# Causal attention with two layer norms: column maxima and sums on VectorE, a third score bank

## The reference, cut to what matters

```python
cq = rms_norm(x @ w_qa.T, q_ln)                       # 2048 x 384
q = (cq @ w_qb.T)                                     # 16 heads x (128 + 64)
ckv = x @ w_kva.T                                     # 128 compressed + 64 rotary
scores = einsum(q_full, k_full) * 192 ** -0.5         # per head 2048 x 2048, causal
attn = softmax(where(causal, -inf, scores))
x = layernorm(x + (attn @ v).reshape(s, H * 128) @ w_o.T)
x = layernorm(x + x @ (weight * scale_weight[:, None]).T + bias)
```

## Time and profile before

| | |
|---|---|
| median of 3 runs | 1709.2 us (1709.2 to 1710.53) |
| profiled execution, its own time | 1709.03 us |
| span of its trace | 1707.2 us |
| TensorE busy | 1648.9 us (97%) |
| VectorE busy | 1399.1 us (82%) |
| ScalarE busy | 1102.1 us (65%) |
| GpSimd busy | 983.7 us (58%) |
| granted TensorE clock | 0.998 |

### The profile page before, as it was taken

The page is one execution under the profiler, slowest core; times in us unless marked ns, Lnnn a source line. Parts: engine busy times, 40 slices in busy tenths (PEclk is TensorE's granted clock), DMA queues, the critical chain, the costliest instruction groups (busy, mean ns, idle before and its releaser), DMA issues. The chain is left out here.

```text
span 1707.2 us, 27648 instructions
## 1 busy us (share of the span) xinstructions
PE 1648.9 (97%) x8405; PEld 1355.0 (79%) x8405; DVE 1399.1 (82%) x2499; ACT 1102.1 (65%) x2064; POOL 983.7 (58%) x937
## 2 busy tenths in 40 slices
PE   7999999999999999999999999999999999999887
PEld 5667788888888888888887878888888788888665
DVE  3565798888888888888888888888888988888895
ACT  4554576666666666766666666766666767666664
POOL 4333465565655556656566555655655665565795
PEclk9999999999999999999999999999999999999999
DMA  7984322212321412223211312123113121111322
GB/s 218 367 319 145 97 68 63 87 58 87 112 79 38 143 37 81 69 80 124 81 56 59 127 58 92 50 81 118 62 63 113 43 70 49 50 44 56 118 95 85
DMA packets 112171, 163.98 MB, mean 96 GB/s; under 512 B 13600, under 2 KB 83488, under 8 KB 109984
## 3 DMA queue, kind: packets, MB, share of 16 engines
q1 hardware_dynamic: 105296, 125.86, 22.9%
q0 software_dynamic: 4864, 16.26, 2.9%
q10 hardware_dynamic: 1872, 20.19, 2.9%
HBM read 101.19 MB, written 61.08 MB: 95 GB/s over the span
## 5 line engine op out<-in xcount | busy, mean ns | idle before, releaser
L1720 POOL TENSOR_TENSOR split_p<-pool,split_p 128x512 fp32r<-128x512 f32 x544 | 708.5, 1304 | 525.4 <-ACT split_p L1616 524.7
L1473 PE MATMUL rows<-q_c,key_c 128*128 128x512 f32 x1632 | 476.1, 400 | 12.3 <-DVE top L1848 11.9
L1604 ACT COPY pool<-rows 128x512 f32<-128x512 f32 x480 | 281.8, 587 | 296.7 <-PE rows L1473 291.0
L1863 DVE TENSOR_TENSOR pool<-bank,pool 128x512 f32<-128x512 f32 x544 | 368.3, 677 | 32.0 <-PE bank L1493 32.0
L1609 ACT ACTIVATE pool<-pool 128x512 f32<-128x512 f32 x544 | 344.8, 634 | 31.3 <-DVE pool L1863 28.3
L1848 DVE TENSOR_TENSOR top<-rows,top 128x512 f32<-128x512 f32 x420 | 288.7, 687 | 85.0 <-ACT pool L1604 81.0
L1616 ACT CAST split_p<-pool 128x512 fp32r<-128x512 f32 x544 | 332.2, 611 | 24.0 <-PE bank L1506 24.0
L1473 PEld LDWEIGHTS rows<-q_c,key_c 128*128 128x128 f32 x1632 | 288.7, 189 | 72.9 <-DVE top L1848 24.9
L1473 PE MATMUL rows<-q_pe,key_pe 128*128 128x512 f32 x1088 | 337.2, 391 | 0.0
L1876 DVE TENSOR_TENSOR bank<-bank,pool 128x512 f32<-128x512 f32 x420 | 289.7, 690 | 0.0
L1473 PEld LDWEIGHTS rows<-q_pe,key_pe 128*128 128x128 f32 x1088 | 204.2, 188 | 45.3
(11 more groups left out here) (190 smaller groups left out, 2021.5 us busy)
## 6 DMA issues: line engine op xcount, KB each, us to landing
q_pe<-pe_dram SPq DMA_DIRECT2D x128, 128.0 KB, 2.6
y_dram<-y SPq DMA_DIRECT2D x62, 256.0 KB, 2.1
cq<-cq_dram SPq DMA_DIRECT2D x19, 768.0 KB, 4.8
y<-y_dram SPq DMA_DIRECT2D x48, 256.0 KB, 3.1
pe_dram<-by_sin SPq DMA_DIRECT2D x32, 256.0 KB, 2.1
pe_dram<-by_cos SPq DMA_DIRECT2D x32, 256.0 KB, 2.2
cq_more<-cq_dram SPq DMA_DIRECT2D x10, 768.0 KB, 4.9
table<-table_dram SPq DMA_DIRECT2D x56, 128.0 KB, 2.8
```

The source lines that it names most:

```text
L1473: mm = pe.matmul(by_head(out), k, q, start=(z == 0), stop=(z == 4))
L1604: nc.scalar.copy(slot(n), SCORES[n % N_SCORES]).then_inc(scores_copied, 1)
L1720: nc.gpsimd.tensor_tensor(split_p[:, n % 2, 1, :], slot(n), stored(split_p[:, n % 2, 0, :]), ALU.subtract).then_inc(p_lo, 1)
L1863: nc.vector.tensor_tensor(slot(n), MAXES, slot(n), ALU.add).then_inc(shifted, 1)
```

## The change

The running total over tiles goes: each tile's exponentials are reduced to 16 columns (4 heads x 4 blocks of 32 queries, each partition holding one query of its block) by a transposing reduction, `parts`, and a short reduction adds the tiles up at the end. The maximum goes the same way: VectorE reduces `top` with a transposing reduction to 16 columns; GpSimd multiplies these by a 0/1 matrix that puts each block of 32 partitions in its own 16 of 64 columns (`widen_max`); TensorE multiplies by the folding matrix, which adds over the blocks and so gives every partition all four values (`fold_max`); VectorE takes the maximum of the four (`join_max`) and spreads it over MAXES by a transpose of 32 x 32 blocks (`spread_max`). The bank of the total becomes a third bank for scores. `top` has one buffer instead of two. All places of steps of the attention are given anew, as 13 x slot + AT; the steps that read a shared bank have places of their own instead of the READ place one slot later. Those of the final linear layer stay.

```diff
-N_SCORES, N_AUX = 2, 3
+N_SCORES, N_AUX = 3, 3
+AT = {'scores': -2, 'max': 7.85, 'shift': -36, 'exp': -22, 'hi': -14, 'sum': -7.75, 'lo': -7.65, 'values': 1, 'reduce_max': 19, 'widen_max': 24, 'fold_max': 38, 'join_max': 46, 'spread_max': -26, 'reduce_sum': 1, 'copy_out': 10, 'fold_sum': 46, 'spread_sum': 38, 'normalise': 33.1, 'o_hi': 51, 'o_lo': 49.25, 'y': 76, 'add_y': 60.15, 'q': 9, 'q_hi': 45.85, 'q_lo': 19.95, 'pe': 6, 'rope': 19.85, 'round_pe': 63, 'store_pe': 58, 'load_pe': 66}
 def timetable():
     for it in range(N_ITER):
         for t in range(keys(it)):
             n, v = number(it, t), value_slot(it, t)
-            yield n, SCORES_AT, ("scores", it, t)
-            yield n, MAX, ("max", it, t)
-            yield v - 3, SHIFT, ("shift", it, t)
-            yield v - 2, EXP, ("exp", it, t)
-            yield v - 1, ROUND, ("hi", it, t)
-            yield v - 1, ROUND, ("sum", it, t)
-            yield v - 1, ROUND, ("lo", it, t)
-            yield v, VALUES, ("values", it, t)
-        e = last_value(it)
-        yield last_slot(it) + 1, USE_AT, ("turn_max", it)
-        yield value_slot(it, 0) - 3, SPREAD, ("spread_max", it)
-        yield e, COPIES, ("reduce_sum", it)
-        yield e + 1, COPIES, ("copy_out", it)
-        yield e, USE_AT, ("fold_sum", it)
-        yield e + 2, READ, ("o_hi", it)
-        yield e + 2, READ, ("o_lo", it)
-        yield e + 4, USE_AT, ("y", it)
+            for what in ("scores", "max"):
+                yield 13 * n + AT[what], 0, (what, it, t)
+            for what in ("shift", "exp", "hi", "sum", "lo", "values"):
+                yield 13 * v + AT[what], 0, (what, it, t)
+        for what in ("reduce_max", "widen_max", "fold_max", "join_max"):
+            yield 13 * last_slot(it) + AT[what], 0, (what, it)
+        yield 13 * value_slot(it, 0) + AT["spread_max"], 0, ("spread_max", it)
+        for what in ("reduce_sum", "copy_out", "fold_sum", "spread_sum", "normalise", "o_hi", "o_lo", "y", "add_y"):
+            yield 13 * last_value(it) + AT[what], 0, (what, it)
...
     elif what == "max":
-        if rest[0] == 1 and it >= 2:
-            yield ("turn_max", it - 2)
+        if rest[0] == 1 and it:
+            yield ("reduce_max", it - 1)
     elif what == "spread_max":
-        yield ("reduce_max", it)
+        yield ("join_max", it)
...
-        OUT, MAXES, TOTAL = m.bank[5:8]
+        SCORES, AUX = [m.bank[n] for n in (0, 1, 5)], m.bank[2:5]
+        OUT, MAXES = m.bank[6:8]
...
-            def turn_max(it):
-                pe.wait_ge(scores_maxed, finished(it))
-                for h in range(HG):
-                    mm = pe.transpose(aux(u)[:, h * P:h * P + P], source[:, h * P:h * P + P], m.ident[:, :])
-            def spread_max(it):
-                for h in range(HG):
-                    mm = pe.transpose(MAXES[:, h * P:h * P + P],
-                                      stats[:, it % 8, h:h + 1].broadcast_to([P, P]), m.ident[:, :])
+            def fold_max(it):
+                pe.wait_ge(max_widened, it + 1)
+                pe.matmul(aux(u)[:, 0:16 * HG], fold[:, :], wide_max[:, it % 2, :], start=True, stop=True
+                          ).then_inc(max_folded, 1)
...
+            def widen_max(it):
+                if it >= 2:
+                    pool.wait_ge(max_folded, it - 1)
+                pool.wait_ge(max_reduced, it + 1)
+                nc.gpsimd.tensor_tensor(wide_max[:, it % 2, :].rearrange("p (a b) -> p a b", a=4),
+                                        part_max[:, it % 2, :].rearrange("p (a b) -> p a b", a=1).broadcast_to([P, 4, 4 * HG]),
+                                        quadrant.rearrange("p (a b) -> p a b", b=1).broadcast_to([P, 4, 4 * HG]), ALU.mult
+                                        ).then_inc(max_widened, 1)
...
             def reduce_max(it):
+                nc.vector.tensor_reduce(part_max[:, it % 2, :], in_blocks(source), AX.X, ALU.max, apply_transpose=True
+                                        ).then_inc(max_reduced, 1)
+            def join_max(it):
+                dve.wait_ge(max_folded, it + 1)
+                nc.vector.tensor_reduce(stats[:, it % 8, :],
+                                        aux(("fold_max", it))[:, 0:16 * HG].rearrange("p (a b) -> p b a", a=4),
+                                        AX.X, ALU.max, negate=True).then_inc(max_done, 1)
+            def spread_max(it):
+                dve.wait_ge(max_done, it + 1)
+                nc.vector.transpose(in_blocks(MAXES),
+                                    stats[:, it % 8, :].rearrange("p (b n) -> p b n", n=1).broadcast_to([P, 4 * HG, 32])
+                                    ).then_inc(max_spread, 1)
...
             def add_up(it, t):
-                if keys(it) == 1:
-                    nc.vector.tensor_copy(TOTAL, slot(n)).then_inc(summed, 1)
-                elif t == 1:
-                    nc.vector.tensor_tensor(TOTAL, slot(n - 1), slot(n), ALU.add).then_inc(summed, 1)
-                elif t > 1:
-                    dve.wait_ge(summed, sums_made(it, t) - 1)
-                    nc.vector.tensor_tensor(TOTAL, TOTAL, slot(n), ALU.add).then_inc(summed, 1)
+                nc.vector.tensor_reduce(parts[:, t, :], in_blocks(slot(n)), AX.X, ALU.add, apply_transpose=True
+                                        ).then_inc(summed, 1)
             def reduce_sum(it):
-                nc.vector.tensor_reduce(row_sum[it % 2], in_blocks(TOTAL), AX.X, ALU.add, apply_transpose=True
+                nc.vector.tensor_reduce(row_sum[it % 2], parts[:, 0:keys(it), :].rearrange("p t b -> p b t"), AX.X, ALU.add
                                         ).then_inc(sum_reduced, 1)
```

More of the change, by code:

```diff
@@ L799, in timetable @@
                 at = 4
-            yield at, USE_AT, use
+            yield 13 * at + AT[use[0]], 0, use
+            if use[0] == "q":
+                yield 13 * at + AT["q_hi"], 0, ("q_hi", *use[1:])
+                yield 13 * at + AT["q_lo"], 0, ("q_lo", *use[1:])
             if use[0] == "pe":
[L802 to L805, removed]
+                yield 13 * at + AT["rope"], 0, ("rope", s + 2)
+                yield 13 * at + AT["round_pe"], 0, ("round_pe", s + 2)
+                yield 13 * at + AT["store_pe"], 0, ("store_pe", s + 2)
+                yield max(13 * at + AT["load_pe"], 13 * (FIRST[2 * s + 2] if s >= 0 else at + 5) + READ), 0, ("load_pe", s + 2)
 def ffn_timetable():
@@ L856, in last_tile @@
     return it, keys(it) - 1
[L859 to L866, removed]
 def waits_for(step):
@@ L913, in waits_for @@
             yield ("o_lo", it - 2)
-    elif what == "turn_max":
+    elif what == "reduce_max":
         yield ("max", *last_tile(it))
-    elif what == "reduce_max":
-        yield ("turn_max", it)
+        if it >= 2:
+            yield ("widen_max", it - 2)
+    elif what == "widen_max":
+        yield ("reduce_max", it)
+        if it >= 2:
+            yield ("fold_max", it - 2)
+    elif what == "fold_max":
+        yield ("widen_max", it)
+    elif what == "join_max":
+        yield ("fold_max", it)
         if it >= 8:
@@ L1023 @@
 PROJECTION_STEPS = [("q", N_PAIR - 1, 0), ("q", N_PAIR - 1, 1)]
-AUX_USES = ("q", "pe", "y", "turn_max", "fold_sum", "turn", "linear")
+AUX_USES = ("q", "pe", "y", "fold_max", "fold_sum", "turn", "linear")
 def plan():
@@ L1045, in plan @@
     at = {}
-    for n, phase, step in itertools.chain(timetable(), ffn_timetable()):
+    for n, phase, step in itertools.chain(timetable(), ((13 * n + phase, 0, step) for n, phase, step in ffn_timetable())):
         at.setdefault((n, phase), []).append(step)
-        for reader in readers(step):
-            at.setdefault((n + 1, READ), []).append(reader)
     for key in sorted(at):
@@ L1112, in attention_phase @@
         o_sum = sb("o_sum", [P, 2, 512])
-        top = sb("top", [P, 2, 512])
+        top = sb("top", [P, 512])
         fold = sb("fold", [P, P])
+        parts = sb("parts", [P, NT, 4 * HG])
         sums = sb("sums", [P, 4, 4 * HG])
@@ L1119, in attention_phase @@
         mask_t = sb("mask_t", [P, P])
[L1120 removed]
+        part_max = sb("part_max", [P, 2, 4 * HG])
+        wide_max = sb("wide_max", [P, 2, 4 * 4 * HG])
+        stats = sb("stats", [P, 8, 4 * HG])
+        quadrant = m.small[:, 52:56]
         row_sum = [sums[:, b, :] for b in range(2)]
@@ L1559, in _ @@
                     scores(*at)
[L1560 to L1563, removed]
+                elif what == "fold_max":
+                    fold_max(*at)
                 elif what == "values":
@@ L1778, in _ @@
                     values_lo(*at)
+                elif what == "widen_max":
+                    widen_max(*at)
                 elif what == "o_lo":
@@ L1977, in _ @@
                     reduce_max(*at)
+                elif what == "join_max":
+                    join_max(*at)
+                elif what == "spread_max":
+                    spread_max(*at)
                 elif what == "shift":
```

63 lines of the change are left out of this document (36 added, 27 removed).

## The result

The changed kernel takes 1647.5 us (median of 4 runs, 1646.0 to 1653.0) against 1709.2 us: ratio 0.9644, 95% interval 0.962 to 0.9667. I had forecast 1676 us with a range of 1652 to 1704.

What follows compares the result with a forecast made beforehand. TensorE was taken to set the time, with VectorE catching up in its bursts. Span 1707.2 - 37.5 (TensorE's work) - 10 (waits gone) + 14 (new waits) = 1673.7, taken to an execution time of 1676 us, range 1652 to 1704.

Steps and rivals of the forecast that it cites:

- TensorE's work, -37.5 us: Turn and spread of the maximum leave TensorE, 59.5 us; a 64-column fold comes, 22 us; bounds 29.5 to 43.5.
- TensorE's waits, -10 + 14 = +4 us: Half of about 20 us of TensorE's waits go; 14 us of new waits come with VectorE at 97%.
- waits vanish too: Rival: VectorE's 22.27 us fits in TensorE's 23.06 an iteration, waits go by 17 us, total 1655 us; chance 0.10.
- VectorE's work, +104 us: Spread, join, sums, closing sum and maximum's first step on VectorE: +1.62 us an iteration, 104 us over 64 iterations.
- Moved places, at nothing (-5 to +8): Later fold of the sums, y's addition, earlier rounding and other moved steps: put at nothing, bounds -5 to +8 us.
- The 2.5 us of waiting before it go: Fold of the sums on TensorE, moved from slot e to e+2: the wait before it, 2.5 us, goes.
- VectorE may lag by one tile more: Third score bank: time to spare for copy and maximum rises from 1.2 to 3.0 us, so VectorE may lag further.
- Reductions from SBUF: no extra: VectorE's new reductions with one SBUF input aren't slowed by GpSimd; no extra time, upper bound 35 us of VectorE work.
- rival of held-up reductions: Rival: GpSimd holds up VectorE's reductions from SBUF, or slots are short; 1695 us (1688 to 1705), chance 0.15.
- GpSimd's product, 0.32 us and hidden: GpSimd's 128x64 product placing row blocks: 0.32 us each, 20 us in all, hidden unless TensorE waits at the fold.
- The slower side, VectorE as the bound: Rival: VectorE's idle time doesn't shrink, being fixed by the order, so VectorE becomes the bound; 1728 us, chance 0.13.
- decisive point: In the VectorE-bound rival: if over 1.7 us of VectorE's 3.35 us idle time an iteration remains, iterations get longer.

Runs made afterwards that it cites:

- a_oldmax: Changed kernel (new places, three banks, new sums) with the old maximum, turned and spread by transposes on TensorE; 1686.1 us, ratio 0.9859 to the kernel before.
- a_dve1: Changed kernel plus one idle copy of the maximum's transposing reduction on VectorE in each iteration; 1663.3 us, ratio 0.9717 to the kernel before.
- a_dve3: Changed kernel plus three idle copies of the maximum's transposing reduction on VectorE in each iteration; 1704.1 us, ratio 0.9960 to the kernel before.
- e_bank: Kernel before with the new sums and the freed bank as third score bank, old maximum, old places; 1701.3 us, ratio 0.9947 to the kernel before.
- b_late3: e_bank with the fold of the sums and its four followers 2.5 slots later; 1682.1 us, ratio 0.9843 to the kernel before.
- e_places: Changed kernel with the old places of all steps that the kernel before had too; 1689.6 us, ratio 0.9864 to the kernel before.
- e_fold: e_places with the fold of the sums and its four followers at their new, later places; 1650.9 us, ratio 0.9654 to the kernel before.
- e_foldhi: e_fold with ScalarE's rounding one tile ahead, behind the copy; 1663.7 us, ratio 0.9729 to the kernel before.
- e_fold2: e_fold with two score banks instead of three; 1692.2 us, ratio 0.9885 to the kernel before.

## Why the prediction was wrong

- **TensorE's work, -37.5 us: right, a little small.** It is -44. The transposes' rounds of 0.93 us from the earlier trace rows held (a_oldmax gives 37 of the 44 back, with less work on VectorE). The fold was mis-sized: 0.24, not 0.35, just below my bound of 0.25. I added two times 0.05 us for the 48 further columns to the 16-column fold, from products that stand in a row by themselves; between other products the wider fold costs no more than the small one.
- **TensorE's waits, -10 + 14 = +4 us: the step that failed.** They fell by 17 to 19, which makes some 22 of the 28 us by which the forecast is too high. Two readings were wrong. I took what there was to gain from the rows of waits of the long stretch, some 20 us, where the spacing of starts says 34, and counted on half of it. And I added 14 us of new waits because VectorE would be at 97%; it is at 93.2%, and none of TensorE's waits for VectorE is left among the rows. In its place stand the third bank and the late fold together, each worth 36 to 40 us when the other is there. The rival "waits vanish too", at -17, has the size by luck: the waits did not vanish, some 44 us of lost starts are left of 61. It misses the time by 7 us, mostly because it has my price of the fold.
- **VectorE's work, +104 us: the term was twice too large.** It is +53.6 us of busy time. By the time each instruction holds the engine until the next one starts, the sums rose by 39 us where I had 56, the join costs 9 where I had 19, and the first step of the maximum became 3 us cheaper where I had 2 dearer. The spread, 46, and the closing sum, -21, came as forecast (49 and -21). The running maximum, the addition of y and others that did not change take some 16 us less. The sums came out lower for this reason: the reduction of a tile is followed by the next instruction after 0.62 us (I had 0.63), but the shift now follows the maximum after 0.58 instead of 0.60, so that a round of shift, sum and maximum takes 1.81 us in both kernels, and the 0.24 us an iteration that I had for this aren't there. a_dve1 and a_dve3 give the price of the rest: by them my 50 us too many would have cost some 18 to 26 us (estimate: over a third to a half), near the 14 us of new waits.
- **Moved places, at nothing (-5 to +8): wrong as a part, right for all but one.** "The 2.5 us of waiting before it go" priced the late fold by the wait that stood there in the kernel before. It is worth 18 us with the old maximum (e_bank to b_late3) and 36 with the new (e_places to e_fold). In the kernel before, the starts lost ahead of this fold were 6 us, in e_places 26. Two banks that held TensorE back first don't explain alone that the wait was short before: with three banks and the old maximum (e_bank) it is 4.6 us. It grows to 26 only when the new maximum joins them, with less work for TensorE and more for VectorE. And part of the gain lies not at the fold but in the low parts, see e_fold. I had named the third bank's 1.2 and 3.0 us to spare, and for the maximum's turn that it wants VectorE at once, but didn't ask the same of the fold of the sums. The other places, y's and the rounding's among them, came to nothing together, as forecast; the rounding's alone cost 13 us (e_foldhi), so their sum at nothing is in part luck.
- **Third bank, "VectorE may lag by one tile more": right, and it needs the late fold.** I gave both together half of 20 us; the bank is worth 40 (e_fold2 to e_fold) with the fold late, and 5 with it early under the old maximum.
- **Reductions from SBUF: no extra, right.** Line 1887 of the kernel after:

```profile
L1887 DVE TRANSPOSE_TENSOR_REDUCE parts<-pool x544: 682/700/714, 178.3 to 1596.7; 128x16 f32<-128x512 f32 x182
```

The longest of 544 is 714 ns, where the two-input addition had one of 1729. The rival of held-up reductions is out. What I had called most plausible for line 1873, a GpSimd instruction in the way, the trace of the kernel before bears out: 7 of its 60 additions took 776 ns or more. All 7 started while a GpSimd instruction was under way, and each ended 0.55 to 0.56 us after that one's end. Of the other 53 only 2 started so. Of the new reductions 421 started while GpSimd was at work, and not one was longer for it. By the rule of the Trainium skill ("SBUF — State Buffer", section "SBUF: two separate sides") an instruction with one SBUF input and in no two-port mode isn't locked out by GpSimd; here the trace agrees, 0 of 544 against 7 of 60. The longest case, before:

```profile
270.22 1.30 POOL L1720 TENSOR_TENSOR split_p<-pool,split_p 128x512 fp32r<-128x512 f32 x1 [0.22 <-ACT split_p L1616]
270.34 1.73 DVE L1873 TENSOR_TENSOR bank<-pool 128x512 f32<-128x512 f32 x1
```
- **GpSimd's product, 0.32 us and hidden: right.** It takes 293 ns (64 of them, 18.8 us), and no wait for the new fold is among TensorE's rows. Only a_dve3 has one, 9.7 us.
- **The slower side, VectorE as the bound: not here.** I set the decisive point at 1.7 us of idle time an iteration; 1.5 remained, with less work than I had reckoned, and TensorE stayed at 99.1%.

## What to carry to other kernels

Read what a wait costs from the spacing of starts, stage by stage, not from the idle time of the rows: here the rows showed 37 of 61 us. Compare two kernels by the same step or by tiles, for 55 against 56 in a stretch is already 0.4 us an iteration. When two engines run one behind the other, list every point where the leading one needs the other's result, with the slots that it may be ahead; a new buffer moves one of these points, and may pay only when the nearest other one moves too, so price them together. A short wait at a place is no proof that the place is harmless, for another limit may stand in front of it.

## What had not been expected of the hardware

The spacing of VectorE's instructions is shorter than their durations and depends on the pair: in the kernel after, the next one follows a transposing reduction (697 ns) after 0.62 us, a shift (679 ns) after 0.60 and a maximum (668 ns) after 0.58. A fold of 64 columns costs TensorE 0.24 us between other products, no more than one of 16 columns (0.25).
